# A macaron block on one core: the fold of the values' weights in half-precision pairs, with its scales found ahead

## What is computed

```python
x = x + 0.5 * ffn(layernorm(x))
x = x + attention(layernorm(x), w_attn, w_o)
x = x + 0.5 * ffn(layernorm(x))

def attention(x, w_attn, w_o):               # windows of 128 tokens, each sees itself and the one before
    q, k, v = split(x @ w_attn.T, 3)         # w_attn 3072x1024
    sim = masked((q / 128) @ k2.T)
    return (square(relu(sim)) @ v2) @ w_o.T  # w_o 1024x1024

def ffn(x):                                  # gate_w, agg_w, bc_w 1024x1024; d1_w 1024x4096; d2_w 4096x1024
    thought = layer_norm(x)[:, -1] @ agg_w + agg_b         # the last token of each sequence alone
    for _ in range(4):
        thought += gelu(layer_norm(thought) @ d1_w + d1_b) @ d2_w + d2_b
    broadcast = thought @ bc_w + bc_b
    gate = sigmoid(x @ gate_w + gate_b)
    return layer_norm(x + gate * broadcast)
```

## Time and profile before

| | |
|---|---|
| median of 3 runs | 2115.98 us |
| the profiled execution | 2117.86 us |
| its span, first to last instruction | 2116.6 us |
| TensorE (PE) busy | 2037.7 us, 96% |
| VectorE (DVE) busy | 1173.0 us, 55% |
| ScalarE (ACT) busy | 664.7 us, 31% |
| DMA engines' mean share | 75.5% |

### The profile page before, as it was taken

One profiled execution on the slowest core, in us unless ns is written; L12 is line 12 of the kernel. 1 busy time (PEld: TensorE's weight loads), 2 busy tenths in 40 slices (PEclk: granted clock), 3 DMA queues, 4 the chain that ended last, 5 costly groups with the idle time before them and its releaser, 6 DMA issues.

```text
span 2116.6 us, 30247 instructions
## 1 busy us (share of the span) xinstructions
PE 2037.7 (96%) x11872; PEld 1037.0 (49%) x11872; DVE 1173.0 (55%) x2108; ACT 664.7 (31%) x931; POOL 159.0 (8%) x281
## 2 busy tenths in 40 slices
PE   8988989999999999998999999999999999999997
PEld 3333433444333446655665555665556564444443
DVE  2321323554344465567676755655555545888887
ACT  0557322433223232222333221211212113444443
POOL 0000000000000010000000000000000000111111
PEclk9999999999999999999999999999999999999999
DMA  8788897988988833348989799898987947555552
GB/s 340 237 311 341 285 353 269 379 319 320 354 338 333 332 132 118 100 140 299 323 294 327 273 320 293 297 347 283 313 290 278 357 149 221 149 151 154 154 149 80
DMA packets 275213, 555.76 MB, mean 263 GB/s; under 512 B 149040, under 2 KB 149248, under 8 KB 274688
## 3 DMA queue, kind: packets, MB, share of 16 engines
q1 hardware_dynamic: 275072, 553.83, 75.5%
HBM read 406.93 MB, written 113.26 MB: 246 GB/s over the span
## 4 chain that ended last, share of the span: by engine, by line
PE 47%; DMA 3%; DVE 2%; SPq 2%; ACT 1%; issue 1%; POOL 0%; ACTq 0%; DVEq 0%
PE product_banks L1023 41%; PE product_banks L1143 3%; PE thought_acc L1208 3%; DMA thought_units<-parts_scratch 1%; DMA gate_arena<-arena 1%; DMA arena<-in_x 0%; SPq L810 0%; DVE thought_units L1754 0%; SPq L944 0%; DMA thought_units<-in_d_w 0%; ACT arena L1315 0%; PE thought_turn L1216 0%; ACT arena L1318 0%; PE thought_acc L1198 0%; DVE arena L1566 0%
## 5 line engine op out<-in xcount | busy, mean ns | idle before, releaser
L1023 PE MATMUL product_banks<-gate_arena,arena 128*128 128x512 f16 x1536 | 354.1, 382 | 0.0
L1023 PE MATMUL product_banks<-wide_a,thought_units 128*128 128x512 f16 x1536 | 331.7, 379 | 0.0
L1023 PE MATMUL product_banks<-gate_arena,wide_a 128*128 128x256 f16 x2688 | 307.5, 274 | 2.4 <-DMA gate_arena<-arena 2.4
L1023 PE MATMUL product_banks<-wide_b,gate_arena 128*128 128x512 f16 x1344 | 301.8, 380 | 0.0
L1023 PEld LDWEIGHTS product_banks<-gate_arena,wide_a 128*128 128x128 f16 x2688 | 260.4, 98 | 59.5 <-issue 28.9
L1054 PE MATMUL product_banks<-wide_a,wide_b 128*128 128x512 f32 x512 | 240.9, 616 | 7.1 <-DMA wide_a<-in_w_attn 6.3
L1023 PEld LDWEIGHTS product_banks<-gate_arena,arena 128*128 128x128 f16 x1536 | 145.0, 98 | 203.6 <-issue 51.0
L1023 PEld LDWEIGHTS product_banks<-wide_a,thought_units 128*128 128x128 f16 x1536 | 150.3, 98 | 181.6 <-DVE arena L1606 0.5
L1023 PEld LDWEIGHTS product_banks<-wide_b,gate_arena 128*128 128x128 f16 x1344 | 127.2, 98 | 167.5 <-issue 24.9
L1423 DVE BATCH_NORM_STATS2 bn_parts<-arena 128x6 f32<-128x512 f32 x256 | 164.3, 684 | 4.4
L1054 PEld LDWEIGHTS product_banks<-wide_a,wide_b 128*128 128x128 f32 x512 | 95.1, 195 | 137.9 <-issue 137.8
(11 more groups left out here) (168 smaller groups left out, 2090.1 us busy)
## 6 DMA issues: line engine op xcount, KB each, us to landing
thought_units<-parts_scratch SPq DMA_DIRECT2D x268, 512.0 KB, 6.1
thought_units<-in_d_w SPq DMA_DIRECT2D x148, 512.0 KB, 6.7
thought_row<-in_d_w SPq DMA_DIRECT2D x76, 512.0 KB, 7.2
arena<-in_x SPq DMA_DIRECT2D x64, 512.0 KB, 8.8
parts_scratch<-thought_units SPq DMA_DIRECT2D x64, 512.0 KB, 6.2
x_scratch<-arena SPq DMA_DIRECT2D x64, 512.0 KB, 6.8
arena<-x_scratch SPq DMA_DIRECT2D x40, 512.0 KB, 6.0
gate_scratch<-arena SPq DMA_DIRECT2D x32, 512.0 KB, 8.3
```

The lines of the kernel that those rows point to most:

```text
L1023: mm = pe.matmul(bank, left(i, k), right(j, k), start=(n == 0), stop=(n == 3 * KD - 1))
```

## The change

- The second fold is made of pairs: three half-precision passes (L1102 in the changed kernel) for each float32 matmul.
- For that both matrices need scales ahead of the fold. 16 pieces `top_rows` load w_o and wv by rows (512 KB each) into three slots of the arena, 16 pieces `top` take their maxima on VectorE (L1531), and `scale_a` and `scale_b` run for each; all of it is paced into the first fold at 1.05. The fourth row's load waits for the first row's maximum, and so on. The gates' bias and the first tile's x, whose places these slots are, are loaded after them.
- `wo_turn` rounds on ScalarE and takes the low half on VectorE (L1538); the bank is free after VectorE. A new piece `wv_split` (8 of them) makes wv's pairs in place, ScalarE (L1335) then VectorE (L1546), one after another.
- The gates' preparations are paced at 0.95 in place of 0.8, with the norms of tiles 0 and 1 ahead of the first turn.
- `gate_save` and the parameters move out of the second fold into the gates behind it, paced between the splits of the folded weights, which go at 0.5 in place of 0.3.
- A piece of the second fold counts 1.28 in place of 1.83 in `time_of`, so the thought's beats come closer together in the rest of the list.
- In the first group the six `v` pieces of its first tile come ahead of `q`; they wait for that tile's transposing DMA alone.

```diff
-        return 1.0 if piece[1:3] == ("qk", 0) else 1.83 * FOLD_SIZES[piece[2]]
+        return 1.0 if piece[1:3] == ("qk", 0) else (1.83 if piece[1] == "qk" else 1.28) * FOLD_SIZES[piece[2]]
...
+        if n == 0:
+            own = [p for p in products if p[0] == "v" and p[2] == 0]
+            products = own + [p for p in products if p not in own]
...
+    tops = [("rest",)] * 4
+    for i in range(2 * KD + 2):
+        tops += [("top_rows", i)] if i < 2 * KD else []
+        tops += [("top", i - 2)] if i >= 2 else []
...
+    tops += [("scale_a", "wv"), ("rest",), ("rest",), ("scale_b", "wv"), ("bias",)]
+    fold_qk = paced(paced(plan_fold("qk"), tops, 1.05, PE_PIECES), gate_rows, 0.95, PE_PIECES)
...
+        if n >= 2:
+            wo.append(("wv_split", n - 2))
+    wo += [("wv_split", KD - 2), ("wv_split", KD - 1)]
...
-    fold_vo = paced(plan_fold("vo"), save, 0.5, PE_PIECES)
+    splits = paced(splits, save, 0.75)
...
-    gates = paced([p for n in range(EARLY, TILES - LATE) for p in plan_gate(n)], splits, 0.3, PE_PIECES)
+    gates = paced([p for n in range(EARLY, TILES - LATE) for p in plan_gate(n)], splits, 0.5, PE_PIECES)
...
+            elif kind == "top_rows":
+                i, = a
+                m, k = divmod(i, KD)
+                if i >= len(top_slots):
+                    was = divmod(i - len(top_slots), KD)
+                    sp.wait_ge(largest[("wo", "wv")[was[0]]], was[1] + 1)
+                sp.dma_start(top_slots[i % len(top_slots)], (w_o, wv)[m][k * P:(k + 1) * P, :]).then_inc(
+                    top_in[i % len(top_slots)], 16)
...
+                        for n, (left, right) in enumerate(((0, wo_high), (0, wo_low), (1, wo_high))):
+                            mm = pe.matmul(bank_ap(key), wv_parts(e)[:, left, d * P:(d + 1) * P],
+                                           right[:, e, h * BANK:(h + 1) * BANK], start=(e == n == 0),
+                                           stop=(e == KD - 1 and n == PARTS - 1))
...
+            elif kind == "top":
+                i, = a
+                m, k = ("wo", "wv")[i // KD], i % KD
+                dve.wait_ge(top_in[i % len(top_slots)], 16 * (i // len(top_slots) + 1))
+                dve.tensor_reduce(scale_stat[m][:, k:k + 1], top_slots[i % len(top_slots)], AX_X, ALU.max,
+                                  apply_absolute_value=True).then_inc(largest[m], 1)
+            elif kind == "wo_turn":
...
+                dve.scalar_tensor_tensor(out=wo_low[place], in0=turn_ap((kind, n, h)).rearrange("p (k t) -> p k t", t=P),
+                                         scalar=scale_stat["wo"][:, KD + 2:KD + 3], in1=wo_high[place], op0=ALU.mult,
+                                         op1=ALU.subtract).then_inc(turn_out[at % TURN_BANKS], 1)
```

More of the change, by code:

```diff
@@ L494, in whole_plan @@
     wo_ahead = 3
-    gate_rows += [("x", 1), ("x", 2)] + [("wo_rows", n) for n in range(wo_ahead)] + [("norm", 0), ("rest",)]
-    gate_rows += [("rest",), ("rest",), ("turn", 0, 0), ("turn", 0, 1), ("norm", 1)]
-    fold_qk = paced(plan_fold("qk"), gate_rows, 0.8, PE_PIECES)
+    gate_rows += [("x", 1), ("x", 2)] + [("wo_rows", n) for n in range(wo_ahead)] + [("rest",)] * 5
+    gate_rows += [("norm", 0), ("rest",), ("norm", 1), ("rest",), ("turn", 0, 0), ("turn", 0, 1)]
+    tops = [("rest",)] * 4
+    for i in range(2 * KD + 2):
+        tops += [("top_rows", i)] if i < 2 * KD else []
+        tops += [("top", i - 2)] if i >= 2 else []
+        if i == 2 * KD:
+            tops.append(("x", 0))
+        if i == KD + 2:
+            tops.append(("scale_a", "wo"))
+        if i == KD + 5:
+            tops.append(("scale_b", "wo"))
+    tops += [("scale_a", "wv"), ("rest",), ("rest",), ("scale_b", "wv"), ("bias",)]
+    fold_qk = paced(paced(plan_fold("qk"), tops, 1.05, PE_PIECES), gate_rows, 0.95, PE_PIECES)
     fold_qk.append(("fold_store", "qk", KD - 1))
@@ L511, in whole_plan @@
         splits += rounded_ahead(m, [("fold_rows", m, k) for k in range(2, KD)])
+    save = [("params",)] + [("rest",)] * 5 + [("half_params",)]
+    for k in range(KD):
+        save += [("gate_save", k)] + [("rest",)] * 3
+    splits = paced(splits, save, 0.75)
     splits += [("prep_fetch", 0), ("rest",), ("rest",), ("prep_norm", 0), ("prep_beta", 0)]
-    gates = paced([p for n in range(EARLY, TILES - LATE) for p in plan_gate(n)], splits, 0.3, PE_PIECES)
+    gates = paced([p for n in range(EARLY, TILES - LATE) for p in plan_gate(n)], splits, 0.5, PE_PIECES)
     out = [("start",)]
@@ L556 @@
     p for p in PLAN if p[0] in ("turn", "wo_turn"))}
-SPLIT_TURN_AT = {piece: n for n, piece in enumerate(
-    p for p in PLAN if p[0] == "turn")}
 MOMENT_AT = {piece: n for n, piece in enumerate(
@@ L561 @@
 SPLIT_AT = {piece: n for n, piece in enumerate(p for p in PLAN if p[0] == "split")}
+SCALE_AT = {piece[1]: n for n, piece in enumerate(p for p in PLAN if p[0] == "scale_b")}
 class Tally:
@@ L716, in macaron_kernel @@
     rounded = sem("rounded")
-    largest = {m: sem(f"largest_{m}") for m in ("gate", "qk", "vo")}
+    largest = {m: sem(f"largest_{m}") for m in SCALE_AT}
+    wv_high, wv_split = sem("wv_high"), sem("wv_split")
     top_found, top_shared = sem("top_found"), sem("top_shared")
```

91 lines of the change are left out of this document (66 added, 25 removed).

## The result

The changed kernel takes 2145.4 us (median of 4 runs, 2138.3 to 2149.0); the kernel before took 2117.5 us on the same chip (4 runs, 2115.5 to 2124.2). The ratio, taken of the means of the runs, is 1.0122, 95% interval 1.0087 to 1.0157: **slower by 1.2%**, where 2094 (2074 to 2114) was forecast. Where two variants ran on different chips, their distance is the difference of their ratios times 2116, good to some 4 us.

The account below looks back on a forecast made before the run. The prediction took TensorE to bound the kernel; its terms, -27.1 + 12.4 - 7.2 + 4 + 3 - 6 + 5 - 6.5 = -22.4, took 2117.9 us to 2095.5, a median of 2094 us (2074 to 2114).

Parts of the forecast that it names:

- The step that failed: Whole kernel: TensorE, busy 2037.7 of 2116.6 us, is the bound, so work taken from it is time saved.
- The fold's term: Second fold: 128 products as three half-precision passes each give back 27.1 us; bounds 27.1 and nothing.
- the rival that something else holds the pace: Second fold: the thought's pairs and stores set its pace, the 27.1 stays as waits; about 2121 us, chance 0.06.
- One sign that the prediction named: Forecast is wrong if TensorE's waits on the thought's loads grow to more than 20 us.
- The maxima ahead: Near 43 us: the thought's variance waits on VectorE behind w_o's first maximum; +12.4 us, bounds 0 and +18.
- The turns of tile 1: Turns of tile 1: TensorE's 5.01 us wait for its norm and slow products go; -7.2 us, bounds 0 and -7.2.
- The turns of w_o: Ahead of the second fold: turn banks wait for ScalarE and VectorE; +3 us, bounds 0 and +8.
- The beats: The thought's beats come closer while its slot ring partly sets the pace; +4 us, bounds 0 and +15.
- Saves and gates: Saves leaving the second fold shorten store waits, -6 us (0 to -9); later loads in the gates, +5 (0 to +20).
- The rival of the DMA engines as the bound: First 750 us: DMA engines become the bound, slower below about 325 GB/s sustained; 2136 us, chance 0.07.
- The first group: Start of the first group: `v` pieces fill the 4.07 us wait for the second tile; -6.5 us, bounds -4 and -7.6.

Follow-up runs that it names:

- all_three: The changed kernel with w_o's and wv's maxima five places later, and beats, saves and splits as before; 2117.7 us, 1.0000 over the kernel before.
- short_fold: The kernel before with three of eight slices of the second fold's sum left out (41 us of TensorE's work); 2106.5 us, 0.9956 over before.
- stores_sooner: all_three with each store of the second fold two pieces sooner in the queue; 2113.6 us, 0.9985 over the kernel before.
- tops_later: The changed kernel with the maxima of w_o and wv begun five places later in the first fold; 2127.4 us, 1.0056 over the kernel before.
- early_tops: four_rows with the maxima of w_o and w_v back at their place of the changed kernel; 2110.3 us, 0.9979 over the kernel before.
- four_rows: stores_sooner with four slots in place of two for the thought's split float32 rows, parameters loaded near the gates' end; 2091.2 us, 0.9887 over before.
- before_four: The kernel before (float32 fold) with values first, stores two pieces sooner and four slots for the split rows; 2102.0 us, 0.9941 over before.
- beats_as_before: The changed kernel with a piece of the second fold counted 1.83 as before; 2135.0 us, 1.0088 over the kernel before.
- close_beats: four_rows with the fold's modelled time as in the changed kernel (1.28), so beats come closer; 2099.0 us, 0.9930 over the kernel before.
- after_four: The changed kernel with four slots for the split rows, maxima, beats, saves and stores unchanged; 2135.1 us, 1.0084 over the kernel before.
- few_tops: The changed kernel with 2 of 16 maxima rows, the scales coming from these alone; 2133.1 us, 1.0079 over the kernel before.

## Why the prediction was wrong

**The step that failed** is the first: "work taken from it is time, as long as nothing else falls due", with the fold at -27.1 and the rival that something else holds the pace at 0.06. The fold's term came true where it was measured (-29.1 of products; stage 108.7 us, forecast 105 to 112). But fold and gates together stay at about 500 us whatever TensorE has to do: 506.7 before, 504.9 after, 498.5 in all_three, 500.1 in short_fold with 41 us less of TensorE's work. In all_three's placings it is the thought's two-slot ring that holds them: four slots give 471.2. In the changed kernel something else holds them as well, since four slots there leave 498.9; that part stays open (below). I read one ring of this chain, the slots that ScalarE frees (95 us of SyncE's waits), and priced it at +4. The ring that binds stood one question further, in what ScalarE itself waited for in the second fold of before, and I had no row of it:

```profile
ACT thought_units L1400 <- DMA thought_row<-in_d_w: 51.8, 13, 7.8
```

The wait of 11.39 us I read as a store's fault; stores_sooner removed the like of it and TensorE still waited 15.5. The rival had the right mechanism but looked for it in the fold alone, whereas in the changed kernel the waits stand in the gates (31.4 us of TensorE's idle time, 6.3 in the fold). I argued against it by throughput, 298 GB/s under 410, and throughput says nothing of a ring that waits for latency. One sign that the prediction named came: TensorE's waits on the thought's loads, up to the end of the gates, are 23.9 us, over the 20 named and 15.2 before.

**The maxima ahead**, +12.4: the first wait was 6.75 us for 6.9 forecast, the landing at 47.06 for 46.5. The small ones didn't come. Missing was the all-reduce on GpSimd, 6.25 us, and the slow stretches were more than the 2.5 us I took. The early place alone costs 14 us (tops_later) to 19 (early_tops), and in four_rows, where the maxima lie later, the fold still begins 9.4 us later than in before_four. Part of these 9.4 is the turns' (+4, next), so the term was by estimate some 19 us (14 and the other 5), a little above its upper bound of 18. I had followed the moved instructions on VectorE and SyncE and not on GpSimd.

**The turns of tile 1**: the wait of 5.01 us went. **The turns of w_o**, +3: the stretch from the first of the seven half turns to the fold is 242.65 to 255.91, 13.3 us for 9.2, +4; VectorE ends most of its waits. Two more waits for VectorE, 3.85 and 2.77 us, stand earlier among the turns, which the term didn't count. In four_rows, spreading these turns gives 5 us in one profile and nothing in the median.

**The beats**, +4 with up to 15: beats_as_before gives 7, close_beats costs 9. Their price is a shift as much as a wait: they come sooner ahead of the fold (against all_three, 485 matmul records up to the end of the first fold for 463), fewer lie beside the second fold (522 for 558), more in the gates (2097 for 2065).

**Saves and gates**: saves out of the fold -6, gates +5 (0 to 20). The fold's part is hardly seen: ScalarE's wait for a store is 6.0 us and not 11.4, but TensorE still waits 3.88 and 2.29 us. The gates, with the beats' share, are +31.2. Undoing the saves gives 7 us in the changed kernel, and in four_rows they cost little. DMA from 0 to 720 us ran at 321 GB/s and not near 345, since nothing in those 720 us got shorter:

```profile
0.00:720.00 720.00, 638.08 (x3205) 253.62 (x3206) 289.23 (x561) 271.24 (x384) 33.17 (x75) 0.95 0.85 321
```

The rival of the DMA engines as the bound gave 2136, near the result, for a wrong reason. Its rule, that the kernel gets slower below 325 GB/s sustained, takes a result for a cause: the kernel before itself moved 325 over these 720 us, and four_rows moves 365 GB/s through the whole fold with the same queue. The Trainium skill, in "HBM Reference", "Specifications (TRN2)", says that a core streaming alone gets about 425 GB/s and only a pair that streams together 358 each; the traces agree, with 410 over 15 us and 365 over the 111 us of four_rows' fold. The 358 that I weighed doesn't bind.

**The first group**, -6.5: -4.2 here and -4.4 alone, at the lower bound. The wait of the earlier trace rows is gone, and the list begins with `v` at 809.5 without one.

**Left open.** From the changed kernel, undoing one part at a time gives 14, 7, 7 and (ring) 8 us, and the stores' place 3 in all_three: 39 of the 50 to four_rows. So some 11 us come only when several parts are undone together, and above all the ring's gain does, 8 us alone and 21 last. Seen from the other end, after_four is 42 us slower than four_rows and differs from it in the three placings and the stores' place. The placings put back one at a time cost 19, 9 and 4; the stores' place was not run with four slots. Of the 28 us that its fold and gates are longer, each single part brings 2 or 3. Which parts together bring the rest, and so what makes the gates of the changed kernel 31 us longer than their work, no run shows; the wait of 9.51 us is one piece of it. Which beats meet which rows was not followed.

## What to carry to other kernels

Don't take an engine that is 96% busy for the bound of a stage until a run with less of its work is shorter by as much: leave a part of the work out, before the rewrite, and see what arrives. Two neighbouring stages whose sum stays while their parts change may have a common pacemaker; look for a ring with few slots and a long round (load, two engines, next load), whose consumer waits often and briefly while the DMA engines are well under their best. And follow each moved instruction on every engine's queue, the ones with few instructions above all.

## What the runs showed of the hardware

- GpSimd's PARTITION_ALL_REDUCE of a 128x1 column has a record of 0.35 us, and GpSimd's next instruction, whose input is there, starts 7.26 us after its start (7.30 in few_tops; 8.37 in early_tops, with a record of 1.30).
- Twice as many slots for one kind of load (and 1 MB less of other loads) took the DMA engines from 316 to 365 GB/s over a stage, 132 us before and 111 after; these loads landed later, at medians of 10.3 to 11.8 us by slot for 7.1, and the stage was shorter all the same.
- Waits of 6 to 7 us cost more than themselves. early_tops reaches the fold 19 us later than four_rows, and 8 of these are the same instructions at a longer busy time (216.7 us for 208.6); its granted clock from 50 to 100 us is 0.88, where four_rows has 1.00.
